# Reading four PSUM banks at once, in place of two, in the first maximum of two long cross attentions

## The reference

```python
q, k, v = x @ Wq.T + bq, context @ Wk.T + bk, context @ Wv.T + bv     # 64, 6272, 6272 rows
attn = softmax(einsum('bihd,bjhd->bhij', q, k) * SCALE)               # over the 6272 keys
x = x + einsum('bhij,bjhd->bihd', attn, v).reshape(...) @ Wo.T + bo
```

## Time and profile before

| | us |
|---|---|
| runs | 662.68, 663.24, 671.8; median 663.24 |
| profiled execution | 663.12 |
| its span, from the first to the last instruction | 661.3 |
| first maximum of level 1, from its first matmul to its last maximum | 161.6 to 182.8 |
| first maximum of level 3, the same | 527.5 to 548.6 |

### The profile page before, as it was taken

The page is one execution under the profiler, slowest core; times in us unless marked ns, Lnnn a source line. Parts: engine busy times, 40 slices in busy tenths (PEclk is TensorE's granted clock), DMA queues, the critical chain, the costliest instruction groups (busy, mean ns, idle before and its releaser), DMA issues. The chain is left out here.

```text
span 661.3 us, 11985 instructions
## 1 busy us (share of the span) xinstructions
PE 513.6 (78%) x4815; PEld 324.5 (49%) x4815; DVE 434.1 (66%) x828; ACT 299.6 (45%) x367; POOL 132.1 (20%) x197
## 2 busy tenths in 40 slices
PE   8799996788889997438995594782578488999857
PEld 5456673575355564313442263472456335556546
DVE  6744325856967955744999999925556596785243
ACT  2578881425557685111654560020112164768611
POOL 2111000000000000204688999400100000000000
PEclk9989997989899999556998587795569679999959
DMA  8364481563200000001022035052300150000000
GB/s 218 72 185 117 128 321 57 173 181 80 94 2 2 1 3 1 3 0 50 0 84 111 0 147 124 5 116 55 127 1 1 31 256 1 2 2 2 2 0 3
DMA packets 17674, 45.59 MB, mean 69 GB/s; under 512 B 4281, under 2 KB 13674, under 8 KB 16778
## 3 DMA queue, kind: packets, MB, share of 16 engines
q1 hardware_dynamic: 17556, 44.72, 22.3%
q0 software_dynamic: 64, 0.11, 0.1%
HBM read 34.28 MB, written 8.29 MB: 64 GB/s over the span
## 5 line engine op out<-in xcount | busy, mean ns | idle before, releaser
L251 POOL TENSOR_TENSOR rstd<-rstd,minus_half 64x1 f32<-64x1 f32 x20 | 11.8, 589 | 420.3 <-DVE rstd L259 420.3
L1497 ACT ACTIVATE ring<-psum,l3x_gain_columns 128x1024 f32<-128x1024 f32 x49 | 54.4, 1114 | 23.2 <-PE psum L1389 23.2
L1497 ACT ACTIVATE ring<-psum,l1x_gain_columns 128x1024 f32<-128x1024 f32 x49 | 54.4, 1114 | 22.4 <-PE psum L1389 22.4
L1403 PE MATMUL psum<-ring,values 128*32 128x128 f32 x1568 | 62.7, 279 | 0.4 <-ACT ring L1497 0.4
L934 ACT ACTIVATE ring<-psum,l0x_key_scale 128x1024 f32<-128x1024 f32 x49 | 52.1, 1114 | 8.2 <-PE psum L827 8.2
L1403 PEld LDWEIGHTS psum<-ring,values 128*32 128x32 f32 x1568 | 37.0, 109 | 28.1 <-issue 24.7
L1602 DVE TENSOR_REDUCE l1x_tops<-psum 128x1 f32<-128x448 f32 x64 | 36.7, 619 | 10.2 <-PE psum L1378 10.1
L1602 DVE TENSOR_REDUCE l3x_tops<-psum 128x1 f32<-128x448 f32 x64 | 36.7, 619 | 10.2 <-PE psum L1378 10.1
L3186 DVE MAX8 l2x_best<-values 128x8 f32<-128x6272 f32 x6 | 40.1, 6691 | 0.1
L3194 DVE MATCH_REPLACE8 values<-l2x_best,values 128x6272 f32<-128x6272 f32 x6 | 40.1, 6675 | 0.0
L827 PE MATMUL psum<-l0x_Q_stack,wide 96*128 96x256 f16 x196 | 29.8, 281 | 4.2 <-ACT ring L934 2.1
(11 more groups left out here) (778 smaller groups left out, 1080.7 us busy)
## 6 DMA issues: line engine op xcount, KB each, us to landing
wide<-keys_aside SPq DMA_DIRECT2D x54, 224.0 KB, 3.8
experts<-in_experts SPq DMA_DIRECT2D x1, 4608.0 KB, 13.5
experts<-in_experts SPq DMA_DIRECT2D x1, 4096.0 KB, 15.3
keys_aside<-ring SPq DMA_DIRECT2D x7, 448.0 KB, 2.5
keys_aside<-experts SPq DMA_DIRECT2D x6, 448.0 KB, 3.2
ring<-in_ctx_tiles SPq DMA_DIRECT2D x1, 2352.0 KB, 9.3
experts<-in_experts SPq DMA_DIRECT2D x1, 2048.0 KB, 7.8
ctx_t<-in_ctx_t SPq DMA_DIRECT2D x3, 672.0 KB, 7.4
```

Source lines behind the costliest of these rows:

```text
L1403: last = nc.tensor.matmul(ps[32 * quarter:32 * quarter + 32, O_BANK, 128 * half:128 * half + 128], mem.values[:, at:at + 32], probs[:, t % ...
L1497: nc.scalar.activation(probs[:, t % PROBS, :].rearrange("p (b n) -> p b n", b=2), ps[:, pair:pair + 2, :], ACT.Exp, scale=exp_gain[:, :]). ...
```

## The change

Each unit becomes one piece. TensorE waits once for all four banks and raises `first_scores` once after the fourth matmul; VectorE reduces four banks (128 x 1792 values) in one instruction; ScalarE copies four banks in one instruction; the counts of all waits follow. The matmuls, the folds, the buffers and the 29 matmuls of `keep_on` are as they were, but `keep_on` waits for the whole last read of s = 0.

```diff
-    def first_read(n, s, p):
+    def first_read(n, s):
         if (n, s) in taken:
-            return first_taken, 2 * taken.index((n, s)) + p + 1
-        return first_copied, 2 * copied.index((n, s)) + p + 1
+            return first_taken, taken.index((n, s)) + 1
+        return first_copied, copied.index((n, s)) + 1
...
                     pe.wait_ge(*stacked_with(u))
+                    if n >= 1:
+                        pe.wait_ge(*first_read(n - 1, s))
                     for g in range(G):
-                        if n >= 1 and g % 2 == 0:
-                            pe.wait_ge(*first_read(n - 1, s, g // 2))
                         last = nc.tensor.matmul(...)
-                        if g % 2 == 1:
-                            last.then_inc(first_scores, 1)
+                    last.then_inc(first_scores, 1)
...
-                pe.wait_ge(*first_read(first[-1][0], 0, 0))
+                pe.wait_ge(*first_read(first[-1][0], 0))
                 keep_on(14)
...
-                    for p in range(2):
-                        act.wait_ge(first_scores, 2 * first.index((n, s)) + p + 1)
-                        bank = s * G + 2 * p
-                        nc.scalar.activation(out[:, 2 * p:2 * p + 2, :], ps[:, bank:bank + 2, 0:HALF], ACT.Identity,
-                                             scale=1.0 / BIAS_ROW).then_inc(first_copied, 1)
+                    act.wait_ge(first_scores, first.index((n, s)) + 1)
+                    nc.scalar.activation(out, ps[:, s * G:(s + 1) * G, 0:HALF], ACT.Identity,
+                                         scale=1.0 / BIAS_ROW).then_inc(first_copied, 1)
...
-                    dve.wait_ge(first_copied, 2 * m + 4)
+                    dve.wait_ge(first_copied, m + 2)
...
-                    for p in range(2):
-                        dve.wait_ge(first_scores, 2 * first.index((n, s)) + p + 1)
-                        v.tensor_reduce(even_tops[:, 2 * p:2 * p + 2, i], ps[:, 2 * p:2 * p + 2, 0:HALF],
-                                        AX_X, ALU.max).then_inc(first_taken, 1)
+                    dve.wait_ge(first_scores, first.index((n, s)) + 1)
+                    v.tensor_reduce(even_tops[:, :, i], ps[:, 0:G, 0:HALF], AX_X, ALU.max).then_inc(first_taken, 1)
...
-                dve.wait_ge(first_taken, 2 * len(taken))
+                dve.wait_ge(first_taken, len(taken))
```

## The result

| | before | after |
|---|---|---|
| median of the runs, us | 664.88 (4 runs, 662.68 to 671.8) | 693.69 (4 runs, 690.01 to 695.52) |
| profiled execution, us | 663.12 | 695.52 |
| span, us | 661.3 | 693.7 |

The ratio of the new kernel to the old is 1.0408, with an interval of [1.0313, 1.0502]. Of 664.88 us that is 27 us (20.8 to 33.4). Ratios, and medians further down, leave out executions more than 1.5% above the fastest of their kernel; ranges in round brackets hold all. The forecast was 680.6 us in a range of 669 to 684. The direction was right, the mechanism of the phase too, but two terms were missing, and the time lies outside the range.

A forecast was written before the change was run, and what follows sets the result against it. VectorE, without a gap in its rounds, was taken to bound the phase. Phases +5.7 and +6.5 us, `keep_on` +2.75 and +2.5, sum 17.5 us on 663.12, gave 680.6 us; range 669 to 684, the forecast's own 679 to 683.

The forecast's parts named there:

- The turns: In the changed phase, TensorE's refill and VectorE's read alternate: rounds of 3.17 us at full, 3.95 us at half clock.
- The clock in the phase: In levels 1 and 3, TensorE busy 81% of a round, so both phases stay at half clock until `keep_on` is dense.
- Rival (a): In both phases, the same turns but half clock only where it is now: sum 8 us, 671.1 us; chance 0.19.
- (b): Clock rises in one level, or midway in both: 12.7 us more, 675.8 us; chance 0.19.
- `keep_on`: Behind the last read, 29 matmuls starting at half clock put the turn 8.1 us behind it: +2.75 and +2.5 us.
- The half clock is free today: In the phase before the change, a round's eight matmuls at half clock take 2.98 us, just fitting VectorE's 3.00.
- a delay of the phase passes to the end one for one: Behind the phase, the softmax loop waits for the turned maxima and is then dense on TensorE, so delays pass unchanged.
- The copy on ScalarE: In each round, ScalarE's four-bank copy takes 1.65 us and costs nothing while VectorE's read is the longer path.
- Rival (c): In the phase, refill hides beside the fold and only shorter reads remain: 0.84 us saved, 662.3 us; chance 0.03.

The follow-up runs named there:

- scalar_four: Only ScalarE's side of the change, query half 1 in one piece, VectorE's query half 0 in two as before; 681.39 us, 1.0242 to the kernel before.
- before, again: The kernel before, unchanged, run once more for a second trace; profiled execution 667.11 us, span 665.2 us.
- vector_four: Only VectorE's side: against the changed kernel, ScalarE's query half 1 in two pieces again; 689.69 us, 1.0367 to the kernel before.
- after_filled: Changed kernel with three matmuls of each unit of query half 1 run twice into the same banks; 677.38 us, 1.0188 to the kernel before.
- before_keep26: Kernel before with 26 in place of 14 matmuls in the first part of `keep_on` in level 1; span 670.4 us.

## Why the prediction was wrong

- **The turns: right.** A round of 3.95 us was worked out, 3.86 measured; a read 2.01 against 2.03 us, a copy 1.65 against 1.66. What was too much is the 0.10 us from matmul to read: the read began 1.69 us behind the first of the four matmuls, which had been put at 1.70 by themselves. The last read ended 6.0 and 6.1 us later than before, counted from the phase's start; 5.7 and 6.5 were forecast.
- **The clock in the phase: right.** Both phases stayed at 0.50 from entry to `keep_on`. Rival (a), the clock as today, and (b), midway, are out for this kernel: in its second trace level 1 entered at full clock, fell at 171.1 and stayed down to `keep_on` as well. The Trainium skill (TensorE: Matmul & The Clock Gate, A second HAM failure mode) tells of a swing; here it was 27.2 us at half without a break (167.6 to 194.8), and of the kernels with a merged hand-over only `scalar_four`, in level 3, has a rise and a fall in the middle of a phase.
- **`keep_on`: right.** The turn came 7.6 and 8.2 us behind the last read (8.1 forecast), +2.25 and +2.6 us (2.75 and 2.5). The range given for it, 7.6 to 8.8, leaves out the turn of 0.14 us that the 8.1 holds.
- **"The half clock is free today": wrong in the first rounds.** It holds for rounds with a fold. The phase of level 1 took 22.4 us with 6.8 us at half, and 21.1 us at full clock throughout (before, again). No term of the sum used it.
- **What lies behind: wrong.** The step that failed is "a delay of the phase passes to the end one for one". I took the loop as dense at full clock and the later stages as fixed. The loop's first part ran at half clock in both levels, +6.0 us, and the stages between took 3.9 us more, of which 3 in a stage that was at half clock once more. These two alone take 680.6 to 690.5 us, above the range; the cause of the 6.0 us is shown, that of the 3.9 in part argued. I had written down that the clock would rise late in `keep_on`, and did not ask what it would be in the sparse stretch that follows.
- **The copy on ScalarE, costed at nothing: wrong by itself, without effect in the sum.** Alone it costs 3.6 and 5.1 us in the phases; beside VectorE's turns it is hidden, as `vector_four` shows.
- **The range was too narrow.** The forecast of 17.45 us for the phases was met by 17.0. The misses stand outside the phase, where I had put no bound at all. The profiled execution lay 14.9 us above the forecast: 6.0 in the loops, 3.9 between, 6.0 in the start, and 1.0 less in the phases and the rest. The start moves by up to 11 us between the traces of this study, and the forecast was built on a trace with one of the earliest; the three runs shown (662.68 to 671.8) had hinted at it.
- **Rival (c), the refill hides: out.** With full clock and a fold beside it the round of `after_filled` was still 3.13 us, against 3.00.

No version of this study beats the kernel before. VectorE had no gap in its rounds with a fold there, so longer reads had no more to win than their own 0.06 us for each pair.

## What to carry to other kernels

A piece-wise hand-over of a buffer is its double buffering: merging two reads, or merely their two events, makes producer and consumer take turns, and costs refill time in each round to save 0.06 us of instruction. Where a matmul engine at half clock just keeps up, a small gap can cost more than itself, since the clock may stay down until the next dense work; and a sum over one phase should carry a term for the clock in the stages behind it.

## What the runs showed of the hardware that was not expected

- With TensorE busy 18.71 of 20.40 us the granted clock stayed at half for the whole stretch (`scalar_four`, level 1). Adding 18 matmuls a level to the changed kernel brought it to full within the phase and saved 16 us by the medians, 12.9 us by the traces without the start (`after_filled`).
- In one trace (`before_keep26`) a turn 1.5 us later in level 1 of the kernel before came with 2.1 us more in the unchanged stages between and 4.9 us more in level 3 (24.7 + 78.0 against 22.6 + 75.2). A second trace of the same kernel was not taken.
- ScalarE's and VectorE's price of a bank in a long instruction followed the line through the shorter ones to 0.02 us.
